# Cross-attention and a routed FFN: GpSimd's expert program unrolled to the indirect transfers alone, ScalarE addressing the bias itself

## The chip, the cores and the metric

One NeuronCore of one Trainium2 chip runs the kernel. The metric is the device time of one execution in microseconds (us). The same kernel was run three times before the change, and the median of these runs is what a changed kernel is held against.

## The reference, cut to what matters

64 sequences of 128 rows with 256 columns pass through two layers. First comes an attention whose softmax runs over the sequences, then a mixture of eight experts, of which each row (token) takes two.

```python
x = x + attention(layernorm(x), ctx_1024, ctx_1024)   # out = v @ softmax(k^T q / 16, over the batch)

# FFN: T = 8192 tokens, H = 256, F = 512, E = 8 experts, K = 2
xn = layernorm(x)
topk_logits, topk_idx = jax.lax.top_k(xn @ router_w.T, 2)
probs = jax.nn.softmax(topk_logits)
hmid = gelu(einsum('th,efh->etf', xn, w1) + b1[:, None, :])
y = einsum('etf,ehf->eth', hmid, w2) + b2[:, None, :]
out = x + einsum('eth,te->th', y, combine)            # combine holds probs at the two chosen experts
```

## The kernel before, in words

The kernel writes a separate program for each engine, and semaphores join the programs. It has three stages: the maximum and the sum of the softmax (two passes over x and ctx), the attention with the second layernorm and the choice of experts, and the experts. The change is in the third stage, and the second one only matters in that it leaves one row of 514 words per token in the DRAM table `rows_first`: the token's x (256 words), its normalized x as two f16 parts, high and low (256 words), and its two probabilities.

**Groups.** The tokens of one expert are padded to groups of 256 (`GROUP`), two tiles of 128 (`SUB`). There are 39 groups for the first choice (round 0) and 39 for the second (round 1), 78 in all (`ALL`). VectorE works out two tables in SBUF: `index`, with four columns for each group (two for the rows to read, two for the rows to write), and `owner_i`, with the expert of each group.

**Steps.** All engines walk through the same steps. In step i they work on different groups, by the lags `L_TR, L_G1, L_G2 = 2, 3, 4`:

- GpSimd (POOL in the profile) issues the two gathers of group i (L532) into one of six pairs of row buffers (`LANES`), then the two scatters of group i-4 (L540), once VectorE has raised `x_sum` for that group. Before a gather it waits until the scatter of group i-6 has landed (`x_out`), since that group had the same buffers.
- TensorE (PE) runs the 24 matmuls of the first layer of group i-3 (L680), the eight transposes of group i-2 (L691) and the 24 matmuls of the second layer of group i-4 (L703), in this order.
- ScalarE (ACT) applies Gelu to group i-3 in four calls (L1059), two after each half of the first layer (`x_hid`), then copies the transposed rows of group i-2 to SBUF as `xT` (L1067). The first layer of the next step waits for that copy.
- VectorE (DVE) splits the Gelu output into a high and a low f16 part (L952, L954), adds the output bias (L941) and adds the second layer's result to the rows (L968), which raises `x_sum`.

**What stands ahead of a gather on GpSimd.** In each step a copy takes four columns of `index` into `ring_idx` (L526), a load reads the group's expert from `owner_i` into a register (L528), and a second copy takes that expert's four bias columns out of `b1T` into `ring_b1` (L529) and raises `x_b1`. The first gather then waits for the first copy. The gathers and scatters take their indices from `ring_idx`. ScalarE waits for `x_b1` and reads its bias at a fixed place in `ring_b1`. TensorE and VectorE already load the expert from `owner_i` themselves (L673, L696, L937).

**Loops.** `expert_steps` writes 6 steps out, loops over five blocks of 6, writes some 12 steps around the middle out, loops over five more blocks and writes the rest out. Inside a loop the group number is a register, so that waits and addresses are computed.

**The middle.** Round 1 reads what round 0 wrote, in the table `rows_second`. The first four groups of round 1 (39 to 42) are gathered from `rows_first` for TensorE's sake. At step 43 GpSimd waits until all scatters of round 0 have landed, and gathers these four groups again from `rows_second` over three steps ("late" gathers, L520), for VectorE's sums.

In step 36 TensorE also runs 64 matmuls that list the tokens of round 1 (L664).

Of the kernel before, what the change touches and what calls it, by code (L numbers as in the profile page):

```python
# [27 lines left out]
I32 = mybir.dt.int32  # L28
U32 = mybir.dt.uint32
ALU = mybir.AluOpType  # L30
ACT = mybir.ActivationFunctionType
# [4 lines left out]
EXPERTS, HID = 8, 512  # L36
# [96 lines left out]
def xattn_ffn(nc, x, ctx, router_w, w1, b1, w2, b2, out):  # L133
# [7 lines left out]
    with ExitStack() as stack:  # L141
# [145 lines left out]
        def take(words, rows=P):  # L287
            taken[0] += words
            return slots[0:rows, taken[0] - words:taken[0]]
# [27 lines left out]
        past = take(ROUNDS * GROUPS * EXPERTS, 1)  # L317
        owner = take(ROUNDS * GROUPS, 1)
        owner_i = take(ROUNDS * GROUPS, 1).bitcast(I32)
        ring_idx = take(LANES * 2 * SUB).bitcast(I32)  # L320
        ring_b1 = take(LANES * FC)
        assert taken[0] <= 28 * 2 * ROW
        b2_all = take(EXPERTS * DIM)
        assert taken[0] <= 28 * 2 * ROW
# [9 lines left out]
        x_rows_in = sems("x_rows_in", LANES)  # L334
        x_late_in = sems("x_late_in", L_G2)
        x_out = sems("x_out", LANES)
        x_idx = sem("x_idx")
        x_b1 = sem("x_b1")
        x_tr = sem("x_tr")
        x_xT = sem("x_xT")  # L340
        x_hid = sem("x_hid")
# [100 lines left out]
        def _(pool):  # L442
# [58 lines left out]

            for r in range(RING):
                pool.wait_ge(a_stored[r], 16 * (PAIRS // RING))
            pool.wait_ge(r_owner, 1)
            pool.wait_ge(r_index, 1)

            def group(i, k, n, rnd):
                if is_step(i, k, GROUPS):
                    pool.wait_ge(r_index, 2)
                if is_step(i, k, GROUPS + L_G2):  # L510
                    for r in range(LANES):
                        pool.wait_ge(x_out[r], 32 * len(range(r, GROUPS, LANES)))
                if isinstance(i, int):

                    for g in late_loads(i + k):
                        r = g % LANES
                        pool.wait_ge(x_rows_in[r], 32 * len(range(r, g + 1, LANES)))
                        pool.wait_ge(x_tr, g + 1)
                        for s in range(SUB):
                            pool.indirect_dma_start(row_buf[r * SUB + s], None, table[1],  # L520
                                                    bass.IndirectOffsetOnAxis(ap=ring_idx[:, r * 4 + s:r * 4 + s + 1], axis=0)).then_inc(x_late_in[g - GROUPS], 16)
                if live(i, k, 0, ALL):
                    g, r = i + k, k % LANES
                    source = table[1] if round_of(i, k, 0, rnd) == 1 and not is_late(g) else table[0]
                    after(pool, x_out[r], n * 32 + k // LANES * 32)
                    pool.tensor_copy(ring_idx[:, r * 4:r * 4 + 4], index[:, bass.ds(g * 4, 4)]).then_inc(x_idx, 1)  # L526
                    pool.wait_ge(x_idx, 1)
                    e = pool.value_load(owner_i[0:1, bass.ds(g, 1)], min_val=0, max_val=EXPERTS - 1)  # L528
                    pool.tensor_copy(ring_b1[:, r * FC:(r + 1) * FC], b1T[:].rearrange("p e f -> p (e f)")[:, bass.ds(e * FC, FC)]).then_inc(x_b1, 1)  # L529
                    wait_apart(pool, x_idx, g + 1)  # L530
                    for s in range(SUB):
                        pool.indirect_dma_start(row_buf[r * SUB + s], None, source,  # L532
                                                bass.IndirectOffsetOnAxis(ap=ring_idx[:, r * 4 + s:r * 4 + s + 1], axis=0)).then_inc(x_rows_in[r], 16)
                if live(i, k, L_G2, ALL):
                    g, r = i + k - L_G2, (k - L_G2) % LANES
                    first = round_of(i, k, L_G2, rnd) == 0
                    wait_apart(pool, x_sum, g + 1)
                    for s in range(SUB):
                        rows = row_buf[r * SUB + s] if first else row_buf[r * SUB + s][:, X2:X2 + DIM]
                        pool.indirect_dma_start(table[1] if first else out_rows, bass.IndirectOffsetOnAxis(ap=ring_idx[:, r * 4 + 2 + s:r * 4 + 3 + s], axis=0), rows, None,  # L540
                                                bounds_check=TOKENS - 1, oob_is_err=False).then_inc(x_out[r], 16)
            expert_steps(pool, group)
            for r in range(LANES):
                pool.wait_ge(x_out[r], 32 * len(range(r, ALL, LANES)))

# [440 lines left out]
        def _(act):  # L986
# [59 lines left out]
            act.activation(b2_all, b2_all, ACT.Copy, scale=WSCALE).then_inc(r_b2s, 1)  # L1046

            act.activation(warm[:], neg_half[:, 0:1], ACT.Gelu)


            def group(i, k, n, rnd):
                if live(i, k, L_G1, ALL):
                    g, r, r2 = i + k - L_G1, (k - L_G1) % LANES, (k - L_G1) % 2
                    act.wait_ge(x_b1, g + 1)
                    after(act, x_low, g * 2 - 2)
                    for f in range(FC):
                        if f % 2 == 0:
                            act.wait_ge(x_hid, g * 2 + f // 2 + 1)
                        last = act.activation(act32[r2][:, f * GROUP:(f + 1) * GROUP], psum[:, 2 + 2 * r2 + f // 2, (f % 2) * GROUP:(f % 2 + 1) * GROUP],  # L1059
                                              ACT.Gelu, bias=ring_b1[:, r * FC + f:r * FC + f + 1], scale=1.0 / WSCALE)  # L1060
                        if f % 2:
                            last.then_inc(x_act, 1)
                if live(i, k, L_TR, ALL):
# [24 lines left out]
```

## Time and profile before

| | us |
|---|---|
| median of 3 runs | 858.28 |
| lowest and highest run | 855.77, 863.21 |
| span of the profiled execution | 909.8 |
| experts' stage in it, from the first gather to the end | 327.2 to 909.8 |

The profiled execution has no time of its own beside its span, which runs from its first to its last instruction. The span is 51.5 us above the median of the runs, so that the profile describes a slower execution than the ones that are timed. Times in the profile count from the start of the span. "Idle before" is the time an engine stood still ahead of an instruction, and the name behind the arrow is what ended it: "issue" means that nothing was waited for that the profile shows, and "remote" that the semaphore was raised later than the end of any instruction that the profile has for it.

### The profile page before, as it was taken

What the parts mean: (1) busy time and instruction counts of PE and PEld (TensorE: products, weight loads), DVE (VectorE), ACT (ScalarE), POOL (GpSimd) and SP (SyncE); (2) the same over time, 40 slices, a digit from 0 to 9 for tenths busy, and PEclk for the clock granted to TensorE, in tenths of its full rate; (3) what the DMA queues carried; (4) which work ended last, traced back from release to release, by engine and by line L of the source; (5) the groups of instructions that cost most, each with busy time, mean ns of one, the idle gap of its engine ahead of it and who ended that gap; (6) DMA issues with size and microseconds to landing.
All of it is one profiled execution on the core that took longest, in us unless ns stands there. A gap on an engine that the chain in (4) does not pass through costs nothing. (4 is left out here: it accounts for less than half of the span.)

```text
span 909.8 us, 22499 instructions
## 1 busy us (share of the span) xinstructions
PE 770.1 (85%) x5931; PEld 649.5 (71%) x5932; DVE 622.8 (68%) x1520; ACT 390.1 (43%) x715; POOL 574.0 (63%) x815
## 2 busy tenths in 40 slices
PE   6999996999996449888989887989588889879886
PEld 5678885878885338766877776978367778767775
DVE  6998999899998758655655654363465656556554
ACT  3555664576666204333333433143133333334331
POOL 5664776788884056666576566366766666665663
PEclk9999997999997559999999999799789999999998
DMA  7887773488885124444344443343533343333330
GB/s 227 251 250 240 237 228 114 137 269 266 267 275 192 53 60 134 131 147 157 118 148 156 142 133 119 112 140 76 159 106 111 106 129 108 97 115 116 96 107 2
DMA packets 82200, 137.20 MB, mean 151 GB/s; under 512 B 10075, under 2 KB 55140, under 8 KB 82032
## 3 DMA queue, kind: packets, MB, share of 16 engines
q0 software_dynamic: 23104, 68.43, 24.9%
q1 hardware_dynamic: 59056, 68.26, 23.9%
q8 instruction: 22, 0.36, 0.2%
q14 instruction: 18, 0.15, 0.1%
HBM read 94.56 MB, written 47.59 MB: 156 GB/s over the span
## 5 line engine op out<-in xcount | busy, mean ns | idle before, releaser
L680 PE MATMUL psum<-work,w1T_high 128*128 128x256 f16 x1248 | 227.4, 285 | 53.5 <-ACT work L1067 36.6
L1059 ACT ACTIVATE work<-psum,slots 128x256 f32<-128x256 f32 x312 | 130.2, 471 | 309.4 <-PE psum L680 233.0
L703 PE MATMUL psum<-w2T_high,slots 128*128 x1248 | 214.7, 277 | 6.2 <-issue 5.1
L680 PEld LDWEIGHTS psum<-work,w1T_high 128*128 x1248 | 124.0, 102 | 85.9 <-issue 67.2
L680 PE MATMUL psum<-work,w1T_low 128*128 128x256 f16 x624 | 177.6, 285 | 3.5 <-issue 3.5
L703 PE MATMUL psum<-w2T_low,slots 128*128 x624 | 172.4, 276 | 1.7 <-issue 1.7
L952 DVE CAST slots<-work 128x512 f16<-128x512 f32 x156 | 71.0, 455 | 138.4 <-ACT work L1059 114.8
L703 PEld LDWEIGHTS psum<-w2T_high,slots 128*128 128x128 f16 x1248 | 119.6, 99 | 23.2 <-issue 9.2
L561 PE MATMUL psum<-slots,work 128*128 (+1 forms) x512 | 124.0, 392 | 7.4 <-ACT slots L991 6.8
L540 POOL DMA_INDIRECT rows_second<-slots x78 | 82.3, 1055 | 66.0 <-issue 35.6
L968 DVE SCALAR_TENSOR_TENSOR slots<-psum,slots 128x256 f32<-128x256 f32 x156 | 68.2, 478 | 78.5 <-remote 63.9
L540 POOL DMA_INDIRECT out_x<-slots x78 | 83.4, 1069 | 57.9 <-issue 44.9
L532 POOL DMA_INDIRECT slots<-rows_first,slots x86 | 90.0, 1047 | 45.8 <-issue 45.6
L561 PEld LDWEIGHTS psum<-slots,work 128*128 128x128 f32 x512 | 94.4, 193 | 32.1 <-issue 15.5
L954 DVE TENSOR_TENSOR slots<-work,slots 128x512 f16<-128x512 f32 x156 | 109.5, 702 | 5.4
L1067 ACT ACTIVATE work<-psum 128x1024 f16<-128x1024 f16 x78 | 80.0, 1026 | 77.3 <-remote 42.2
L532 POOL DMA_INDIRECT slots<-rows_second,slots x70 | 71.6, 1022 | 38.4 <-issue 38.4
L941 DVE SCALAR_TENSOR_TENSOR slots<-slots 128x256 f32<-128x256 f32 x156 | 69.2, 485 | 25.9 <-issue 21.3
L680 PEld LDWEIGHTS psum<-work,w1T_low 128*128 x624 | 63.8, 102 | 15.0 <-issue 5.5
L703 PEld LDWEIGHTS psum<-w2T_low,slots 128*128 128x128 f16 x624 | 61.8, 99 | 11.8 <-issue 4.1
L633 PE MATMUL psum<-slots,work 128*128 (+1 forms) x256 | 65.5, 400 | 4.3 <-DVE slots L832 4.3
L691 PE MATMUL psum<-ident,slots 128*128 128x128 f16 x624 | 50.9, 224 | 19.8 <-DMA slots<-rows_first,slots 11.5
(126 smaller groups left out, 1125.2 us busy)
## 6 DMA issues: line engine op xcount, KB each, us to landing
work<-in_ctx SPq DMA_DIRECT2D x96, 256.0 KB, 3.5
rows_first<-slots SPq DMA_DIRECT2D x32, 514.0 KB, 3.9
slots<-in_x SPq DMA_DIRECT2D x32, 256.0 KB, 3.8
work<-in_L_ffn_w SPq DMA_DIRECT2D x32, 256.0 KB, 3.2
work<-in_x SPq DMA_DIRECT2D x32, 256.0 KB, 3.1
slots<-rows_first,slots POOLq DMA_INDIRECT x86
rows_second<-slots POOLq DMA_INDIRECT x78
slots<-rows_second,slots POOLq DMA_INDIRECT x78
```

What stands on the lines that cost most here:

```text
L532: pool.indirect_dma_start(row_buf[r * SUB + s], None, source, bass.IndirectOffsetOnAxis(ap=ring_idx[:, r * 4 + s:r * 4 + s + 1], axis=0)). ...
L540: pool.indirect_dma_start(table[1] if first else out_rows, bass.IndirectOffsetOnAxis(ap=ring_idx[:, r * 4 + 2 + s:r * 4 + 3 + s], axis=0), ...
L561: mm = pe.matmul(psum[:, r2, h * DIM:(h + 1) * DIM], ctx_ring[:, place, h * P:(h + 1) * P], slot(b, 0, DIM), start=True, stop=True)
L633: mm = pe.matmul(psum[:, 2 + r, j * DIM:(j + 1) * DIM], a_ctxT[:, 2 * r + j, h * P:(h + 1) * P], slot(m * 2 + j, h * DIM, DIM), start=(h = ...
L680: mm = pe.matmul(h, w1T[pw][:, f, c, bass.ds(e * P, P)], xT[r2][:, (px * HC + c) * GROUP:(px * HC + c + 1) * GROUP], start=(c == 0 and px ...
L703: mm = pe.matmul(y, act16[r2][pa][:, f * GROUP + s * P:f * GROUP + (s + 1) * P], w2T[pw][:, f, bass.ds(e * DIM, DIM)], start=(f == 0 and p ...
L941: last = dve.scalar_tensor_tensor(rows[:, X2:X2 + DIM], b2_all[:, bass.ds(e * DIM, DIM)], rows[:, PR + now:PR + now + 1], rows[:, X2:X2 + ...
L952: dve.tensor_copy(act16[r2][0][:, cols], act32[r2][:, cols]).then_inc(x_high, 1)
L954: dve.tensor_tensor(act16[r2][1][:, cols], act32[r2][:, cols], act16[r2][0][:, cols], ALU.subtract).then_inc(x_low, 1)
L968: last = dve.scalar_tensor_tensor(rows[:, X2:X2 + DIM], psum[:, 6 + r2, s * DIM:(s + 1) * DIM], rows[:, PR + now:PR + now + 1], rows[:, X2 ...
L1059: last = act.activation(act32[r2][:, f * GROUP:(f + 1) * GROUP], psum[:, 2 + 2 * r2 + f // 2, (f % 2) * GROUP:(f % 2 + 1) * GROUP], ACT.Ge ...
L1067: act.activation(xT[r2], psum[:, 0, :].bitcast(F16), ACT.Copy).then_inc(x_xT, 1)
```

## The change

- GpSimd's program for the experts is written out for all 82 steps, with no loop and no register. The two copies (L526, L529), the expert's load (L528) and the buffers `ring_idx` and `ring_b1` are gone. Gathers and scatters read their indices from `index` in place. The order of gathers, scatters and late gathers is the same.
- ScalarE loads the expert from `owner_i` for each group and addresses the bias in `b1T` by that register. Its wait for `x_b1` is gone. Ahead of the stage it waits once for `owner_i` and `b1T`.
- GpSimd no longer waits for `r_owner`; the semaphores `x_idx` and `x_b1` are gone.

```diff
-            def group(i, k, n, rnd):
-                if is_step(i, k, GROUPS):
+            def gather(g, s, source, landed_on):
+
+                pool.indirect_dma_start(row_buf[g % LANES * SUB + s], None, source,
+                                        bass.IndirectOffsetOnAxis(ap=index[:, g * 4 + s:g * 4 + s + 1], axis=0)).then_inc(landed_on, 16)
+
+            for step in range(ALL + L_G2):
+                if step == GROUPS:
                     pool.wait_ge(r_index, 2)
...
-                if live(i, k, 0, ALL):
-                    g, r = i + k, k % LANES
-                    source = table[1] if round_of(i, k, 0, rnd) == 1 and not is_late(g) else table[0]
-                    after(pool, x_out[r], n * 32 + k // LANES * 32)
-                    pool.tensor_copy(ring_idx[:, r * 4:r * 4 + 4], index[:, bass.ds(g * 4, 4)]).then_inc(x_idx, 1)
-                    pool.wait_ge(x_idx, 1)
-                    e = pool.value_load(owner_i[0:1, bass.ds(g, 1)], min_val=0, max_val=EXPERTS - 1)
-                    pool.tensor_copy(ring_b1[:, r * FC:(r + 1) * FC], b1T[:].rearrange("p e f -> p (e f)")[:, bass.ds(e * FC, FC)]).then_inc(x_b1, 1)
-                    wait_apart(pool, x_idx, g + 1)
+                if step < ALL:
+                    g = step
+                    after(pool, x_out[g % LANES], g // LANES * 32)
                     for s in range(SUB):
-                        pool.indirect_dma_start(row_buf[r * SUB + s], None, source,
-                                                bass.IndirectOffsetOnAxis(ap=ring_idx[:, r * 4 + s:r * 4 + s + 1], axis=0)).then_inc(x_rows_in[r], 16)
+                        gather(g, s, table[1] if g >= GROUPS + L_G2 else table[0], x_rows_in[g % LANES])
...
             def group(i, k, n, rnd):
                 if live(i, k, L_G1, ALL):
                     g, r, r2 = i + k - L_G1, (k - L_G1) % LANES, (k - L_G1) % 2
-                    act.wait_ge(x_b1, g + 1)
+                    e = act.value_load(owner_i[0:1, bass.ds(g, 1)], min_val=0, max_val=EXPERTS - 1)
                     after(act, x_low, g * 2 - 2)
...
-                                              ACT.Gelu, bias=ring_b1[:, r * FC + f:r * FC + f + 1], scale=1.0 / WSCALE)
+                                              ACT.Gelu, bias=b1T[:].rearrange("p e f -> p (e f)")[:, bass.ds(e * FC + f, 1)], scale=1.0 / WSCALE)
```

GpSimd's program in one step of the first loop, before. L526 to L529 are the copies and the expert's load ("TENSOR_LOAD slots" reads `owner_i`, which lies in the tensor `slots`), L532 the gathers, L540 the scatters.

```order
L526 COPY slots<-slots 128x4
L528 ISA
L528 TENSOR_LOAD slots
L528 ISA x2
L529 ISA
L529 COPY slots<-b1T 128x4
L118 REGISTER_ALU
L532 DMA slots<-rows_first,slots 128x514 x2
L118 REGISTER_ALU
L540 DMA rows_second<-slots 8192x514 x2
```

GpSimd's program from the start of the stage, after. L504 is the gather and L529 the scatter.

```order
L504 DMA slots<-rows_first,slots 128x514 x10
L529 DMA rows_second<-slots 8192x514 x2
L504 DMA slots<-rows_first,slots 128x514 x2
L529 DMA rows_second<-slots 8192x514 x2
L504 DMA slots<-rows_first,slots 128x514 x2
```

Nothing but the four transfers of a step is left, and the scatters of one step are followed directly by the gathers of the next.

ScalarE's program in one step of the first loop, before. L1059 is Gelu, L1067 the copy to `xT`.

```order
L1058 REGISTER_ALU
L1059 ACTIVATE work<-psum,slots 128x256 x2
L1058 REGISTER_ALU
L1059 ACTIVATE work<-psum,slots 128x256 x2
L1065 REGISTER_ALU
L111 ISA
L1067 ACTIVATE work<-psum 128x1024
```

ScalarE's program in one step of the first loop, after. L1049 is Gelu, L1057 the copy to `xT`, L1044 the expert's load.

```order
L1044 ISA
L1044 TENSOR_LOAD slots
L1044 ISA x2
L1048 REGISTER_ALU
L1049 ISA
L1049 ACTIVATE work<-psum,b1T 128x256
L1049 ISA
L1049 ACTIVATE work<-psum,b1T 128x256
L1048 REGISTER_ALU
L1049 ISA
L1049 ACTIVATE work<-psum,b1T 128x256
```

The load of the expert has moved from GpSimd to ScalarE, where it stands behind the copy to `xT` of the step before, and each Gelu has an address instruction ahead of it.

## Rows read from the trace of the kernel before

**Rows 1.** The page's first part: busy time, share of the span, instructions.
```profile
PE 770.1 (85%) x5931; PEld 649.5 (71%) x5932; DVE 622.8 (68%) x1520; ACT 390.1 (43%) x715; POOL 574.0 (63%) x815
```
**Rows 2.** Groups by line: POOL's of the experts (busy, mean ns, idle before).
```profile
L532 POOL DMA_INDIRECT slots<-rows_first,slots x86 | 90.0, 1047 | 45.8 <-issue 45.6
L532 POOL DMA_INDIRECT slots<-rows_second,slots x70 | 71.6, 1022 | 38.4 <-issue 38.4
L540 POOL DMA_INDIRECT rows_second<-slots x78 | 82.3, 1055 | 66.0 <-issue 35.6 <-DVE slots L968 30.4
L540 POOL DMA_INDIRECT out_x<-slots x78 | 83.4, 1069 | 57.9 <-issue 44.9 <-DVE slots L968 13.0
```
**Rows 3.** Timeline of POOL from 505 us: start, length, line, idle before.
```profile
505.02 1.02 POOL L540 DMA_INDIRECT rows_second<-slots  x1 [1.90 <-DVE slots L968]
506.35 1.00 POOL L540 DMA_INDIRECT rows_second<-slots  x1 [0.30 <-issue]
507.34 0.21 POOL L526 COPY slots<-slots 128x4 int32 x1
507.47 0.20 POOL L529 COPY slots<-b1T 128x4 f32 x1
508.39 1.00 POOL L532 DMA_INDIRECT slots<-rows_first,slots  x1 [0.72 <-issue]
...
513.29 0.30 POOL L526 COPY slots<-slots 128x4 int32 x1
```
**Rows 4.** Timeline of TensorE, 502 to 508 us.
```profile
502.24 0.39 PE L680 MATMUL psum<-work,w1T_high 128*128 128x256 f16 x2 [1.26 <-ACT work L1067]
...
507.93 0.27 PE L680 MATMUL psum<-work,w1T_high 128*128 128x256 f16 x1
```
**Rows 5.** Timeline of POOL: first and last of 42 scatters right behind a gather.
```profile
357.91 1.02 POOL L540 DMA_INDIRECT rows_second<-slots  x1 [0.31 <-issue]
...
875.58 1.02 POOL L540 DMA_INDIRECT out_x<-slots  x1 [0.30 <-issue]
```
**Rows 6.** Waits from 337 to 906 us: engine, line, releaser, us, times, longest.
```profile
DVE slots L968 <- remote: 63.9, 22, 6.0
ACT work L1059 <- remote: 56.3, 15, 11.5
ACT work L1067 <- remote: 42.2, 22, 3.7
PE psum L680 <- ACT work L1067: 35.4, 20, 3.3
```
**Rows 7.** The source view of L532: who waited for the gathers.
```profile
  PE psum L691: 17.0, 2
```
**Rows 8.** Timeline of POOL: the first gather, and a scatter of the last steps.
```profile
327.21 1.23 POOL L532 DMA_INDIRECT slots<-rows_first,slots  x1 [0.78 <-issue]
...
889.76 1.00 POOL L540 DMA_INDIRECT out_x<-slots  x1 [5.55 <-DVE slots L968]
```
**Rows 9.** Timeline of POOL in the middle: the first late gather, the next gathers.
```profile
631.74 0.99 POOL L520 DMA_INDIRECT slots<-rows_second,slots  x1 [2.01 <-issue]
...
655.14 0.97 POOL L532 DMA_INDIRECT slots<-rows_second,slots  x1 [0.81 <-issue]
```
**Rows 10.** The source views of L937 and L941: VectorE's load of the expert.
```profile
L937 DVEq TENSOR_LOAD <-slots x78: 300/306/590, 342.6 to 897.7; - x78
L941 DVEq FUSED_REGOPS  x78: 69/75/76, 343.5 to 898.3; - x78
```
**Rows 11.** Timeline of ScalarE, 505 to 510 us.
```profile
505.80 1.02 ACT L1067 ACTIVATE work<-psum 128x1024 f16<-128x1024 f16 x1
509.44 0.84 ACT L1059 ACTIVATE work<-psum,slots 128x256 f32<-128x256 f32 x2 [2.62 <-issue]
```
**Rows 12.** The page's third part: a queue, its packets, MB, share of 16 engines.
```profile
q8 instruction: 22, 0.36, 0.2%
```
**Rows 13.** Timeline of VectorE, 505 to 507 us.
```profile
505.94 0.43 DVE L952 CAST slots<-work 128x512 f16<-128x512 f32 x1 [0.16 <-ACT work L1059]
```

More of the change, by code:

```diff
@@ L319, in xattn_ffn @@
         owner_i = take(ROUNDS * GROUPS, 1).bitcast(I32)
-        ring_idx = take(LANES * 2 * SUB).bitcast(I32)
-        ring_b1 = take(LANES * FC)
         assert taken[0] <= 28 * 2 * ROW
@@ L336, in xattn_ffn @@
         x_out = sems("x_out", LANES)
-        x_idx = sem("x_idx")
-        x_b1 = sem("x_b1")
         x_tr = sem("x_tr")
@@ L503, in _ @@
                 pool.wait_ge(a_stored[r], 16 * (PAIRS // RING))
-            pool.wait_ge(r_owner, 1)
             pool.wait_ge(r_index, 1)
-            def group(i, k, n, rnd):
-                if is_step(i, k, GROUPS):
+            def gather(g, s, source, landed_on):
[3 more added lines that the diff above has]
+                if step == GROUPS:
@@ L509, in group @@
                     pool.wait_ge(r_index, 2)
-                if is_step(i, k, GROUPS + L_G2):
+                if step == GROUPS + L_G2:
                     for r in range(LANES):
                         pool.wait_ge(x_out[r], 32 * len(range(r, GROUPS, LANES)))
[L513 to L521, printed above, removed]
@@ L534, in group @@
[L534 to L537, printed above, removed]
+                for g in late_loads(step):
+                    pool.wait_ge(x_rows_in[g % LANES], 32 * (g // LANES + 1))
+                    pool.wait_ge(x_tr, g + 1)
+                    for s in range(SUB):
+                        gather(g, s, table[1], x_late_in[g - GROUPS])
+                if step < ALL:
+                    g = step
+                    after(pool, x_out[g % LANES], g // LANES * 32)
+                    for s in range(SUB):
+                        gather(g, s, table[1] if g >= GROUPS + L_G2 else table[0], x_rows_in[g % LANES])
@@ L538, in group @@
+                if step >= L_G2:
+                    g = step - L_G2
+                    r, first = g % LANES, g < GROUPS
+                    pool.wait_ge(x_sum, g + 1)
                     for s in range(SUB):
                         rows = row_buf[r * SUB + s] if first else row_buf[r * SUB + s][:, X2:X2 + DIM]
-                        pool.indirect_dma_start(table[1] if first else out_rows, bass.IndirectOffsetOnAxis(ap=ring_idx[:, r * 4 + 2 + s:r * 4 + 3 + s], axis=0), rows, None,
+                        pool.indirect_dma_start(table[1] if first else out_rows, bass.IndirectOffsetOnAxis(ap=index[:, g * 4 + 2 + s:g * 4 + 3 + s], axis=0), rows, None,
@@ L541, in group @@
                                                 bounds_check=TOKENS - 1, oob_is_err=False).then_inc(x_out[r], 16)
-            expert_steps(pool, group)
             for r in range(LANES):
@@ L1048, in _ @@
             act.activation(warm[:], neg_half[:, 0:1], ACT.Gelu)
+            act.wait_ge(r_owner, 1)
+            act.wait_ge(s_setc, 1)
             def group(i, k, n, rnd):
```

## The prediction, made before the changed kernel was run

> **What bounds the kernel now.** I read four views, in this order: the page's busy shares, the groups by line, the timelines of single engines in the experts' stage, and the waits of that stage.
>
> The shares name TensorE (85%) and leave GpSimd at 63% [rows 1]. That is an average over three stages and does not count issue time. The experts' stage runs from GpSimd's first gather at 327.2 us [rows 8] to the end of the span at 909.8, so it is almost two thirds of the time. In it two engines have to be held against the number of steps, 78.
>
> TensorE: where nothing holds it up, one step takes 507.93 - 502.24 = 5.69 us, from the first matmul of one first layer to that of the next [rows 4].
>
> GpSimd: the groups by line give four transfer calls a step, of (90.0 + 71.6 + 82.3 + 83.4) / 312 = 1.05 us on average [rows 2]. Between two calls without a wait lie 0.30 us [rows 3]. Between a scatter's end and the next gather lie the copies and the load: from 507.35 to 508.39, 1.04 us [rows 3]. As a mean over all steps: the idle time before gathers is 45.8 + 38.4 = 84.2 us; 78 second gathers take 0.30 each, 23.4, which leaves 60.8 / 78 = 0.78 before a first gather, and the two copies ahead of it span 0.33 (507.34 to 507.67) [rows 2, 3]. That is 1.11 us. So GpSimd's own work in a step is 4 x 1.05 + 3 x 0.30 + 1.11 = 6.21 us. The shortest step that rows show is 513.29 - 507.34 = 5.95 [rows 3]. GpSimd, with its low busy share, needs half a microsecond more for a step than TensorE.
>
> Does it set the pace? In the profiled execution only partly. 78 steps of 6.21 and eight late gathers of some 1.3 (the first one starts at 631.74) [rows 9] are 495 us, out of 582.6 from 327.2 to the end. In 42 of 78 steps the first scatter starts 0.30 us behind the gather, which means that VectorE's sum had been ready and GpSimd was the late one [rows 5]; in the others GpSimd waited, as in the 1.90 us ahead of 505.02 [rows 3]. TensorE itself waited for gathered rows only 17.0 us in two places [rows 7]. What lengthens the other steps are "remote" waits: 63.9, 56.3 and 42.2 us on VectorE and ScalarE, each for a result of TensorE [rows 6].
>
> *The Trainium skill, "Perfetto Trace Analysis", section on the TensorE instruction, says that the end of a matmul in the profile is estimated and its semaphore is raised when PSUM has acknowledged the writes. By that rule a remote wait is a real lateness of TensorE that its rows hide. The trace agrees in so far as the waiting engines do start late; whether the runs without a profiler have it, no page tells.*
>
> Here I have to choose. The runs are 51.5 us shorter than the profiled span. I take most of that to come out of the remote waits (162.4 us in sum, in parts beside each other). GpSimd's stage is 582.6 us with 495 of own work, 88 of waiting. Take 51.5 off, and 36 us of waiting are left. Some 20 of these are at the two ends and in the middle, where it must wait for others anyway (2.01 before the first late gather, 5.55 at 889.76) [rows 8, 9]. So in the timed runs GpSimd would be late in nearly every step, at 6.21 + 16 / 74 = 6.4 us a step.
>
> **The change part by part.**
>
> *Copies, load and the wait ahead of a gather go.* Of the 1.11 us between a scatter and a gather 0.30 stay. GpSimd saves 0.81 us a step, 63 us over 78, and its own step becomes 4 x 1.05 + 4 x 0.30 = 5.40 us. Nothing new is waited for: `index` is complete before the first gather. What is late next is TensorE, at 5.69. So a step in which GpSimd set the pace gains 6.21 - 5.69 = 0.52 us and not 0.81. Where GpSimd was not late, the step gains nothing. Steps that gain: at least the 42 that the trace shows, 42 x 0.52 = 22 us; at most some 72 (all but those at the ends), 37 us. I take 24, near the lower end, because 42 is what was seen and because small waits stay that two engines of nearly equal pace (5.40 and 5.69) cause each other.
>
> *The middle.* After the barrier GpSimd does six transfers a step for three steps; the gather of group 45 starts at 655.14 us, 23.4 after the first late one [rows 9]. Each of these steps is GpSimd's own and gains the whole 0.81: 2.4 us.
>
> *The first gather.* One copy pair and load ahead of the first gather go, about 1 us. I count 0 to 1 and take 0.5.
>
> *ScalarE's load of the expert.* The trace has no such load on ScalarE, but VectorE has the same one: 0.306 us, and 0.19 in the middle of its register operations, which do not occupy the engine [rows 10]. It stands behind the copy to `xT` and ahead of the next Gelu. Between the end of that copy at 506.82 and the next Gelu at 509.44 ScalarE stood still for 2.62 us [rows 11]. That gap hides it: cost 0. If the cover were gone, it would be 0.5 us in each step, 39 us. TensorE's next step waits for the copy, which is ahead of the load, so I see nothing that would take the cover away.
>
> *Four bias addresses.* An address operation takes 0.075 us on VectorE [rows 10]. It stands between the wait and the Gelu, so each half starts some 0.1 later; queued behind the second half is the copy to `xT`, and TensorE waits for that. The copy ended at 506.82 and TensorE began at 507.93 [rows 4, 11]: 1.1 us of cover in an undisturbed step. In the 20 places where TensorE did wait for the copy [rows 6] it is not covered: 20 x 0.1 = 2 us, at most 20 x 0.2 = 4. Below nothing only by the wait for `x_b1` that goes; its copy is made three steps ahead, so 0. I take 1.5, since fewer such places are left in the timed runs.
>
> *The loop on GpSimd goes.* Its program grows from blocks of 24 transfers to some 320 in a row, and has to be fetched. The instruction queue moved 22 packets in 0.2% of 16 engines' span [rows 12]: 0.002 x 909.8 x 16 / 22 = 1.3 us each, an estimate. Some 20 more, each waited for in full, would be 26 us; each beside a running call, nothing. Each call is 1 us of cover and the fetch is in sequence. I take 0 and keep 26 as the far end.
>
> *VectorE's casts beside denser calls.* A cast starts at 505.94 [rows 13], inside the scatter call that ran from 505.02 and took 1.02 us; the next call took 1.00 [rows 3]. So I add nothing.
>
> *The Trainium skill, "SBUF — State Buffer", "SBUF: two separate sides", says that GpSimd cannot write transfer descriptors while VectorE runs a copy that takes the shared port. By that rule two casts of 0.455 us a step would stretch GpSimd's step from 5.40 to 6.3 us and leave no gain. The trace speaks against it here: the call with a cast inside it and the call behind it have one length.*
>
> **The sum.** 24 + 2.4 + 0.5 - 1.5 = 25.4 us less. From the median of 858.3: **833 us**. For the profiled execution, whose span is 909.8, the same sum gives 884.
>
> **The rivals.**
>
> *The change is hidden (no change).* If the 51.5 us between profile and runs lie somewhere else, TensorE's late results set the pace in the runs too, and GpSimd only follows. For it: TensorE waited for rows just twice [rows 7], and where GpSimd waited it could be for 1.9 us, with nothing of its own late [rows 3]. Against it: a late GpSimd in 42 steps. Left would be the middle, 2.4 + 0.5 - 1.5: 857 us.
>
> *All of it falls to TensorE (a larger gain).* If the remote waits are the profiler's alone, every step comes down from 6.4 to 5.69: 0.7 x 72 = 50 us, less the small waits: 815 us. Against it: two engines 0.3 us apart do not run without waits.
>
> *The transfers get in TensorE's way (slower).* ScalarE's copy had 22 remote waits with 42.2 us, 1.9 each [rows 6]. They occur in the stage in which GpSimd issues transfers without end, and today a pause of 1.1 us parts the calls in each step; without it four and more stand together. Against it speaks only that no row ties a late result to a transfer. If the density of transfers is what makes TensorE late, and not the profiler, the 36 steps that were spared get such a wait, 36 x 1.9 = 68 us, of which the 25 of the gain and some 1.1 us of cover a step (40) are to be taken off: about 3 us; if the cover is used up already, which the profiled mean of 582.6 / 78 = 7.5 us a step suggests, it is +15 to +25. It decides from the point where a step's wait exceeds the 0.5 us of gain. Time: 875 us.
>
> **How the numbers follow.** Forecast (GpSimd's pace gives way to TensorE's, 822 to 846): 0.58. Hidden: 0.20. Larger gain: 0.10. Slower: 0.12, in which I count the fetch of instructions. About 1% is what a measurement of this kernel tells from no change. Faster by over 1% (below 849.7): 0.58 + 0.10 + a little of the hidden case, 0.70. Slower by over 1%: 0.10. Within: 0.20. The range reaches from the larger gain to the hidden case with its spread: 816 to 862; beyond it lie most of the slower case and the lowest of the larger one.
>
> **What would show it.** Right: no copies on GpSimd, 0.30 us between every scatter and the next gather, waits for VectorE ahead of most scatters, and more TensorE steps of 5.69. ScalarE's load between copy and Gelu with no later start of the copy. Wrong: gaps of GpSimd over 0.30 with "issue" that come at regular places (fetching), calls longer than 1.05 (the port), remote waits of over 162 us in sum (density), or a first layer that starts later behind ScalarE's copy.

## The result, and the profile after

| | kernel before | changed kernel |
|---|---|---|
| median, us | 857.81 (855.77 to 863.21, 4 runs) | 813.97 (811.98 to 817.22, 4 runs) |
| ratio of the times | | 0.9483, 95% interval 0.9443 to 0.9524 |
| profiled execution: time, span | no time, 909.8 | 815.25, 813.4 |

The change saves 43.8 us, about 5%. 833 us was predicted, with a range of 816 to 862: the direction was right, the size too small, and the result lies 2 us below the range.

The page of the changed kernel, its shares and its groups of GpSimd (to be held against [rows 1, 2]), and the two queues that fetch instructions (the first is that of [rows 12]):

```profile
PE 742.4 (91%) x5931; PEld 647.9 (80%) x5932; DVE 618.6 (76%) x1520; ACT 386.7 (48%) x716; POOL 538.4 (66%) x658
...
L504 POOL DMA_INDIRECT slots<-rows_first,slots x86 | 89.2, 1038 | 61.5 <-DVE slots L901 35.7
L529 POOL DMA_INDIRECT rows_second<-slots x78 | 83.3, 1068 | 56.1 <-issue 34.8
L529 POOL DMA_INDIRECT out_x<-slots x78 | 82.2, 1054 | 42.1 <-issue 32.1
L504 POOL DMA_INDIRECT slots<-rows_second,slots x78 | 77.6, 995 | 25.5 <-issue 24.2
```

```profile
q8 instruction: 22, 0.36, 0.2%
q14 instruction: 19, 0.16, 0.1%
```

The calls are as long as before (1.04 us on average, 1.05 before), and GpSimd has 157 instructions less (815 to 658). One instruction queue has 22 packets in every kernel of this study; the other has 19 here, and 18 in both traces of the kernel before. The idle time ahead of second-table gathers fell from 38.4 us for 70 calls to 25.5 for 78 (here the eight late gathers are among them). Of the 61.5 us ahead of first-table gathers, 35.7 are one wait for VectorE's tables ahead of the stage, which in the kernel before stands ahead of the first copy. The idle time ahead of scatters is now GpSimd's slack.

The timeline of the changed kernel's POOL from 499 us (as [rows 3]):

```profile
499.77 1.00 POOL L529 DMA_INDIRECT rows_second<-slots  x1 [0.30 <-issue]
501.07 0.99 POOL L504 DMA_INDIRECT slots<-rows_first,slots  x1 [0.30 <-issue]
502.37 0.98 POOL L504 DMA_INDIRECT slots<-rows_first,slots  x1 [0.30 <-issue]
503.86 1.05 POOL L529 DMA_INDIRECT rows_second<-slots  x1 [0.50 <-issue]
```

0.30 us stand between a scatter and the next gather where [rows 3] has 1.04. The idle time has moved ahead of the first scatter (0.50 here; on average, by the groups above, 56.1 + 42.1 less 78 x 0.30, over 78: 0.96 us), where GpSimd waits for `x_sum`. GpSimd now waits for the others.

TensorE's timeline shows the pace. The first rows of the first layers of two neighbouring steps, and between them the transposes that follow the first one:

```profile
501.87 0.38 PE L668 MATMUL psum<-work,w1T_high 128*128 128x256 f16 x2
...
504.49 0.61 PE L679 MATMUL psum<-ident,slots 128*128 128x128 f16 x8
...
507.56 0.38 PE L668 MATMUL psum<-work,w1T_high 128*128 128x256 f16 x2
```

507.56 - 501.87 = 5.69 us, the undisturbed step of [rows 4], and no row between them has an idle time. Taken over the whole stage (the start of each first layer less the start of the one before), only 6 of the 77 differences are over 5.75 us, and every other one is 5.69.

The waits of the changed kernel between 337 and 810 us (as [rows 6]):

```profile
ACT work L1049 <- PE psum L668: 259.9, 155, 14.8
...
POOL rows_second L529 <- issue: 34.8, 75, 1.0
...
PE psum L668 <- ACT work L1057: 1.2, 1, 1.2
```

There is no remote wait, and TensorE waits once, 1.2 us, for ScalarE's copy; it waited 20 times and 35.4 us in [rows 6]. This raised the first question, whether [rows 6] describes the runs that were timed.

### The profile page after: what moved, and what is told of

Its sections match the earlier page's. It is cut to its first block and busy times, and to the rows that moved or that the text cites. A ratio compares the mean times of both kernels' runs of the same rounds, so it can differ in the third digit from the quotient of the medians.

```text
span 813.4 us, 22177 instructions
## 1 busy us (share of the span) xinstructions
PE 742.4 (91%) x5931; PEld 647.9 (80%) x5932; DVE 618.6 (76%) x1520; ACT 386.7 (48%) x716; POOL 538.4 (66%) x658
## 5 line engine op out<-in xcount | busy, mean ns | idle before, releaser
L1049 ACT ACTIVATE work<-psum,b1T 128x256 f32<-128x256 f32 x312 | 130.7, 470 | 260.0 <-PE psum L668 259.9
L668 PE MATMUL psum<-work,w1T_high 128*128 128x256 f16 x1248 | 213.3, 276 | 2.5 <-ACT work L1057 2.5
L691 PE MATMUL psum<-w2T_high,slots 128*128 x1248 | 211.1, 275 | 0.5 <-issue 0.5
L668 PE MATMUL psum<-work,w1T_low 128*128 128x256 f16 x624 | 172.4, 276 | 0.0
L940 DVE CAST slots<-work 128x512 f16<-128x512 f32 x156 | 68.8, 441 | 118.8 <-ACT work L1049 118.7
L504 POOL DMA_INDIRECT slots<-rows_first,slots x86 | 89.2, 1038 | 61.5 <-DVE slots L901 35.7
L529 POOL DMA_INDIRECT rows_second<-slots x78 | 83.3, 1068 | 56.1 <-issue 34.8
L942 DVE TENSOR_TENSOR slots<-work,slots 128x512 f16<-128x512 f32 x156 | 108.6, 696 | 5.4
L529 POOL DMA_INDIRECT out_x<-slots x78 | 82.2, 1054 | 42.1 <-issue 32.1
L1057 ACT ACTIVATE work<-psum 128x1024 f16<-128x1024 f16 x78 | 79.8, 1023 | 32.0 <-PE psum L679 32.0
L504 POOL DMA_INDIRECT slots<-rows_second,slots x78 | 77.6, 995 | 25.5 <-issue 24.2
L929 DVE SCALAR_TENSOR_TENSOR slots<-slots 128x256 f32<-128x256 f32 x156 | 68.8, 483 | 27.7 <-DMA slots<-rows_second,slots 13.4
L668 PEld LDWEIGHTS psum<-work,w1T_low 128*128 x624 | 61.9, 99 | 7.9
L478 POOL TENSOR_TENSOR smax<-slots,smax 128x768 f32<-128x768 f32 x31 | 52.3, 1686 | 19.1 <-ACT slots L986 17.2
```

The lines of the kernel that those rows point to most:

```text
L504: pool.indirect_dma_start(row_buf[g % LANES * SUB + s], None, source, bass.IndirectOffsetOnAxis(ap=index[:, g * 4 + s:g * 4 + s + 1], axis ...
L668: mm = pe.matmul(h, w1T[pw][:, f, c, bass.ds(e * P, P)], xT[r2][:, (px * HC + c) * GROUP:(px * HC + c + 1) * GROUP], start=(c == 0 and px ...
L691: mm = pe.matmul(y, act16[r2][pa][:, f * GROUP + s * P:f * GROUP + (s + 1) * P], w2T[pw][:, f, bass.ds(e * DIM, DIM)], start=(f == 0 and p ...
L929: last = dve.scalar_tensor_tensor(rows[:, X2:X2 + DIM], b2_all[:, bass.ds(e * DIM, DIM)], rows[:, PR + now:PR + now + 1], rows[:, X2:X2 + ...
L940: dve.tensor_copy(act16[r2][0][:, cols], act32[r2][:, cols]).then_inc(x_high, 1)
L942: dve.tensor_tensor(act16[r2][1][:, cols], act32[r2][:, cols], act16[r2][0][:, cols], ALU.subtract).then_inc(x_low, 1)
```

## The experiments

The predicted mechanism was that GpSimd saves the time of its two copies and the load. The rivals that were tested behind it are that the loop with its registers costs the time, and that the wait between the copies and the gather does. The latter is what later expectations call Theory 3: GpSimd's sequencer needs some 0.8 us to prepare an indirect transfer, does so while the previous one runs, and is kept from it by a wait that stands as an instruction of its own. In the diffs `index` and `ring_idx` stand for the full index expressions.

### The kernel before, traced again

No edit.

> The kernel before, unchanged, for a second trace. Theory A (the remote waits come from the profiler, not from the kernel): the span is again near 910 us, 50 us above the timed runs, with some 160 us of remote waits. Theory B (the traced execution of before was an odd one): the span is within 1% of the timed runs, 850 to 865 us, and the remote waits are a small part of the 162 us. Under B the step that is neither held by a remote wait would take GpSimd's own 6.2 us nearly everywhere.

Measured: 860.39 us, span 858.6, beside 859.55 for the runs of before on the same chip. Its waits from 337 to 855 us:

```profile
ACT work L1059 <- PE psum L680: 290.0, 156, 15.5
...
DVE slots L968 <- PE psum L703: 42.3, 53, 2.7
```

Its POOL, 507 to 512 us:

```profile
507.15 1.01 POOL L540 DMA_INDIRECT rows_second<-slots  x1 [0.30 <-issue]
508.47 1.00 POOL L540 DMA_INDIRECT rows_second<-slots  x1 [0.30 <-issue]
509.46 0.29 POOL L526 COPY slots<-slots 128x4 int32 x1
509.71 0.18 POOL L529 COPY slots<-b1T 128x4 f32 x1
510.84 1.00 POOL L532 DMA_INDIRECT slots<-rows_first,slots  x1 [0.96 <-issue]
```

And the first rows of two of its first layers on TensorE:

```profile
500.48 0.38 PE L680 MATMUL psum<-work,w1T_high 128*128 128x256 f16 x2
...
506.80 0.38 PE L680 MATMUL psum<-work,w1T_high 128*128 128x256 f16 x2
```

What follows. The trace that the prediction was read from shows an odd execution: no remote wait appears here, and the span agrees with the timed runs. Theory B holds. Here the scatter comes 0.30 us behind the gather in 72 of the 74 steps that have both, not in 42 (the same count in the first trace): GpSimd is late nearly everywhere, and a step takes 506.80 - 500.48 = 6.32 us. Of that, 0.96 us are a gap in which GpSimd does nothing that the profile shows, behind two copies that together span 0.43; the median of this gap over the 78 steps is 0.72. Over all steps scatter end to gather is 1.21 us on average.

The sum of what TensorE's steps take over 5.69 us is 65.1 us in this trace and 23.6 in the changed kernel's, and the difference, 41.5, is nearly the whole gain. It lies in two places:

| us over 5.69 in TensorE's steps | before, traced again | changed |
|---|---|---|
| first step | 1.5 | 1.6 |
| two steps at the listing of step 36 | 13.7 | 13.2 |
| three steps of the middle | 15.2 | 8.7 |
| all other 71 steps | 34.6 (48 of them over 5.75) | 0 |

The 48 steps lose 0.72 us each. They are fewer than the 72 in which GpSimd is late: TensorE runs eight steps of 5.69 us behind the first one and seven behind the listing, until GpSimd's lead is used up.

### The copies kept, the program written out

The changed kernel with both copies, the load and ScalarE's bias as before. The wait carries a constant.

```diff
+                    pool.tensor_copy(ring_idx, index).then_inc(x_idx, 1)
+                    e = pool.value_load(owner_i[0:1, bass.ds(g, 1)], min_val=0, max_val=EXPERTS - 1)
+                    pool.tensor_copy(ring_b1, b1T of expert e).then_inc(x_b1, 1)
+                    pool.wait_ge(x_idx, g + 1)
```

> GpSimd's program is written out for all steps, but keeps both copies and the expert's load; ScalarE as before. Theory 1 (what counts is GpSimd's own work in a step, 6.2 us against TensorE's 5.69): no gain, 850 to 860 us. Theory 2 (the loop with its registers and branches is what costs): most of the gain is there, under 835 us.

Measured: 818.73 us, ratio 0.9534 (0.9499 to 0.957). Its POOL from 511 us:

```profile
511.86 0.27 POOL L527 COPY slots<-slots 128x4 int32<-128x4 int32 x1
512.08 0.18 POOL L529 COPY slots<-b1T 128x4 f32 x1
512.41 1.01 POOL L509 DMA_INDIRECT slots<-rows_first,slots  x1 [0.15 <-issue]
```

What follows. By the recorded alternatives this is Theory 2, the loop; the runs below show that it is not the loop. It falsifies the prediction's reading of the gap. All that GpSimd was to be relieved of is still there, and so is most of the gain: 859.55 - 818.73 = 40.8 us of 43.8. The copies still span 0.40 us, but the gather comes 0.15 behind them instead of 0.96 (0.72 in [rows 3]; the medians over 78 steps are 0.16 and 0.72); the mean from scatter to gather is 0.64. GpSimd's own step is then 4 x 1.05 + 3 x 0.30 + 0.64 = 5.74 us, as good as TensorE's 5.69.

### The loop kept, one copy and the load off GpSimd

The kernel before with the bias on ScalarE as in the changed kernel.

```diff
-                    e = pool.value_load(owner_i[0:1, bass.ds(g, 1)], min_val=0, max_val=EXPERTS - 1)
-                    pool.tensor_copy(ring_b1, b1T of expert e).then_inc(x_b1, 1)
...
-                    act.wait_ge(x_b1, g + 1)
+                    e = act.value_load(owner_i[0:1, bass.ds(g, 1)], min_val=0, max_val=EXPERTS - 1)
```

> GpSimd keeps its loop and the copy of the indices with its wait; the bias copy and the load go and ScalarE addresses the bias itself, as in the changed kernel. Theory 1: GpSimd saves the 0.13 to 0.2 us that the second copy adds behind the first, 10 to 15 us over 78 steps: 842 to 850 us. Theory 2 (the load in front of the gather is the costly part): GpSimd's gap from scatter to gather falls below 0.7 us and the time below 830 us. A theory in which ScalarE's part costs: slower than the kernel with everything on GpSimd, over 858 us.

Measured: 854.46 us, ratio 0.9936 (0.9903 to 0.9969). Its POOL, 510 to 513 us:

```profile
510.97 0.29 POOL L526 COPY slots<-slots 128x4 int32 x1
512.11 1.15 POOL L530 DMA_INDIRECT slots<-rows_first,slots  x1 [0.84 <-POOL slots L526]
```

What follows. None of the three recorded alternatives came (842 to 850, under 830, over 858 us). One of the two copies and the load went, and the gap stayed: 0.84 us behind the one copy that is left, and 1.20 from scatter to gather on average against 1.21. The gain is 0.6%, less than the forecast held to be told from no change, though the interval leaves 1 out.

### The program written out, with the index copy alone

The changed kernel with the first copy and its wait put back; ScalarE as in the changed kernel.

```diff
+                    pool.tensor_copy(ring_idx, index).then_inc(x_idx, 1)
+                    pool.wait_ge(x_idx, g + 1)
```

> The changed kernel with the copy of the indices and its wait put back, so that GpSimd's program is unrolled and each first gather waits for one small copy. Theory 1: the gap from scatter to gather is again about 0.9 us, GpSimd's step 6.0, and the time 840 to 850 us. Theory 2 (loop or load are what costs): within 5 us of 814.

Measured: 817.48 us, ratio 0.9517 (0.9486 to 0.9548). Its POOL from 510 us:

```profile
510.67 0.49 POOL L527 COPY slots<-slots 128x4 int32<-128x4 int32 x1
511.43 1.00 POOL L509 DMA_INDIRECT slots<-rows_first,slots  x1 [0.27 <-POOL slots L527]
```

What follows. Against the run before it the work is the same (index copy, wait, gather), only the loop is missing, and 0.27 us stand where 0.84 stood. So it is the loop, or something that comes with it. In the loop a wait against a register is made of two lines, `eng.wait_ge(sem, 1)` and `eng.wait_ge(sem, count)` in `wait_apart` (L118 to L121), and one of the two stands in the program as an instruction of its own, while the gather carries the other. In the trace of the kernel of 854.46 us the own instruction starts 33 to 35 ns behind the end of the index copy in all 78 steps, so it is the one that the copy holds up. From the end of the copy to the gather it is never under 0.82 us there (median 0.84); in this kernel, where the gather carries the only wait, the median is 0.28. The before kernel has it in its written-out steps too, and the gap with it ([rows 9]: 0.81 at 655.14).

### The same with one more wait line, still no loop

The first kernel with the copies kept (818.73 us), with one line added. It changes nothing that is computed or waited for, since the second line asks for at least as much.

```diff
                     pool.tensor_copy(ring_b1, b1T of expert e).then_inc(x_b1, 1)
+                    pool.wait_ge(x_idx, 1)
                     pool.wait_ge(x_idx, g + 1)
```

> The unrolled program with both copies (e1), but ahead of the gather the wait for the index copy stands twice, so that one of the two is a sequencer instruction of its own, as in the kernel before. Theory 3 (the kernel before lost its time to that wait of its own: GpSimd's sequencer prepares a transfer for some 0.8 us, and behind a wait of its own it can begin only when the copy is done): the gap from scatter to gather goes from 0.64 back to 1.2 us, GpSimd's step to 6.2 to 6.4, and the time to 845 to 862 us, although nothing is looped. Theory 2 (loop, registers and branches): 815 to 822 us, as e1.

Measured: 858.18 us, ratio 0.9972 (0.995 to 0.9994), against 0.9534 without the line. Its POOL from 511 us:

```profile
512.22 0.30 POOL L527 COPY slots<-slots 128x4 int32<-128x4 int32 x1
512.47 0.18 POOL L529 COPY slots<-b1T 128x4 f32 x1
513.37 1.10 POOL L509 DMA_INDIRECT slots<-rows_first,slots  x1 [0.72 <-issue]
```

The source view of the wait's line in this kernel (median ns, first and last start), an instruction of GpSimd's sequencer that the kernel without the extra line has nowhere:

```profile
L531 POOLq EVENT_SEMAPHORE  x78: 17/17/17, 326.7 to 831.0; - x78
```

What follows. One wait line 78 times brings the whole cost back: 0.9972 - 0.9534 = 0.0438 of 859 us, 38 us, or half a microsecond a step. The instruction takes 17 ns by the profile; the price is in the gap behind it, 0.72 us where 0.15 stood (1.23 on average from scatter to gather, 0.64 without the line). This program has no loop and no branch, and its group numbers are constants, so none of these costs anything that the runs can tell.

### The wait moved ahead of the bias copy

The kernel before; the wait for the index copy stands between the two copies, so that the bias copy stands behind it and can run beside the preparation.

```diff
-                    pool.tensor_copy(ring_b1, b1T of expert e).then_inc(x_b1, 1)
                     wait_apart(pool, x_idx, g + 1)
+                    pool.tensor_copy(ring_b1, b1T of expert e).then_inc(x_b1, 1)
```

> The kernel before with its loop; the wait for the index copy is moved from the gather to the bias copy that stands ahead of it, so that the gather carries no wait. Theory 3: the wait is still a sequencer instruction of its own ahead of the gather, so the 0.8 us of preparation still follow it: gap 1.1 to 1.3 us, 850 to 862 us. A theory in which only a wait that the gather itself carries costs: gap near 0.6, under 830 us.

Measured: 866.3 us, ratio 1.0085 (1.0056 to 1.0113). Its POOL from 510 us:

```profile
510.47 0.29 POOL L526 COPY slots<-slots 128x4 int32 x1
510.99 0.51 POOL L530 COPY slots<-b1T 128x4 f32 x1 [0.23 <-POOL slots L526]
511.99 1.50 POOL L532 DMA_INDIRECT slots<-rows_first,slots  x1 [0.49 <-issue]
```

What follows. Behind the wait everything starts over: 0.23 us until the bias copy starts, which is now longer, and 0.49 more to the gather. From the end of the index copy, where the wait is met, to the gather it is 511.99 - 510.76 = 1.23 us, more than the 1.09 (509.75 to 510.84) of the kernel before. Part of the preparation hides under the copy (0.49 against 0.96), but the chain is longer. On average scatter end to gather is 1.36 us against 1.21. So a wait that the gather doesn't carry costs as well when another instruction stands between; the recorded range (850 to 862 us, a gap of 1.1 to 1.3) was missed by 4 us: it did not count that the bias copy would wait and take longer.

### ScalarE's load twice

The changed kernel with the expert's load written twice on ScalarE.

```diff
                     e = act.value_load(owner_i[0:1, bass.ds(g, 1)], min_val=0, max_val=EXPERTS - 1)
+                    e = act.value_load(owner_i[0:1, bass.ds(g, 1)], min_val=0, max_val=EXPERTS - 1)
```

> The changed kernel with ScalarE's load of the expert made twice in each step. If the load is hidden behind the wait for TensorE, as the prediction put it: 812 to 817 us, no change. If ScalarE's added instructions are on the path: 0.5 us in each of 78 steps, 850 us.

Measured: 815.92 us, ratio 0.9485 (0.9442 to 0.9528); the changed kernel has 0.9483. The source view of the load in the changed kernel, and of the bias addresses:

```profile
L1044 ACTq TENSOR_LOAD <-slots x78: 273/286/594, 334.2 to 794.4; - x78
```

```profile
L1049 ACTq FUSED_REGOPS  x312: 46/46/52, 338.1 to 799.7; - x156
```

And the idle time ahead of Gelu, first in the changed kernel, then with two loads:

```profile
503.48 0.84 ACT L1049 ACTIVATE work<-psum,b1T 128x256 f32<-128x256 f32 x2 [2.62 <-PE psum L668]
```

```profile
504.85 0.84 ACT L1050 ACTIVATE work<-psum,b1T 128x256 f32<-128x256 f32 x2 [2.63 <-PE psum L668]
```

What follows. The load is hidden in ScalarE's wait for TensorE, even a second time: 2.62 and 2.63 us, as in [rows 11]. This half of the change costs nothing.

### Waits that are always met

The changed kernel, with two waits ahead of each gather for semaphores that were raised long before.

```diff
                     g = step
                     after(pool, x_out[g % LANES], g // LANES * 32)
+                    pool.wait_ge(r_index, 1)
+                    pool.wait_ge(r_owner, 1)
```

> The changed kernel with two more waits ahead of each gather, on semaphores that were raised long before the stage, so that waits of their own stand ahead of the gather but are met at once. Theory 3 (a wait of its own costs only by what the sequencer can't prepare while it stands at it): no gap over 0.30 us is added, 812 to 818 us. A theory in which a wait instruction ahead of a transfer costs by itself: GpSimd's gap grows by some 0.8 us, 845 us or more.

Measured: 815.15 us, ratio 0.9479 (0.9425 to 0.9533). Its POOL from 504 us:

```profile
504.69 1.17 POOL L531 DMA_INDIRECT rows_second<-slots  x1 [0.30 <-issue]
506.17 1.00 POOL L504 DMA_INDIRECT slots<-rows_first,slots  x1 [0.30 <-issue]
```

What follows. The trace has one wait instruction a step here (78), so a wait of its own is there; it is already met and passes while a scatter runs. It costs nothing, and the gather comes 0.30 us behind the scatter. The cost needs both: the wait as an instruction of its own ahead of the transfer, and a semaphore that is raised only by the work just issued.

### Can the rest be had? The late gathers, one group a step

What the changed kernel's TensorE still loses is in the middle and at the listing (below). In the middle GpSimd does six transfers a step for three steps. The changed kernel was given one late group in each of four steps instead.

```diff
-            first = step - L_G2 + (step > GROUPS + L_G2)
-            return [g for g in range(first, step - L_G2 + 2) if is_late(g) and step >= GROUPS + L_G2]
+            return [g for g in (step - L_G2,) if is_late(g)]
```

> The changed kernel with the four late gathers one per step (steps 43 to 46) instead of two in step 43 and one each in 44 and 45; an attempt at a faster middle. If the 9 us that the middle costs over TensorE's own steps come from the gather of group 43 standing behind four late transfers: 2 to 4 us less, 810 to 812. If they come from GpSimd's six transfers a step as such: no change, 812 to 817. If group 40's late rows are what TensorE waits for: 2 to 4 us more.

Measured: 828.82 us, ratio 0.965 (0.9619 to 0.9681), 14.9 us slower than the changed kernel. Its POOL in the middle:

```profile
590.51 1.22 POOL L528 DMA_INDIRECT out_x<-slots  x1 [3.74 <-issue]
...
613.29 1.27 POOL L528 DMA_INDIRECT out_x<-slots  x1 [3.79 <-issue]
```

The same stretch in the changed kernel:

```profile
592.80 1.28 POOL L529 DMA_INDIRECT out_x<-slots  x1 [1.11 <-issue]
...
600.87 1.02 POOL L529 DMA_INDIRECT out_x<-slots  x1 [0.30 <-issue]
```

What follows. None of the recorded sizes came (2 to 4 us either way, or no change). GpSimd stands 3.7 to 4.1 us before the scatters of four steps: with one late group a step, its rows are fetched in the very step that needs them. The rows of the scatter say only "issue"; who waits for the late rows is VectorE, three times with up to 7.7 us, as the waits of this kernel from 580 to 620 us have it (13.4 us in the same window of the changed kernel), and the scatters wait for VectorE's sums:

```profile
DVE slots L928 <- DMA slots<-rows_second,slots: 22.7, 3, 7.7
```

Six transfers in a row, all 0.30 us apart, are the better order. No version here beats the changed kernel.

## Why the prediction was wrong in size and right in direction

**The term that was mis-sized** is the first one of the sum: "at least the 42 that the trace shows, 42 x 0.52 = 22 us; at most some 72, 37 us. I take 24". The table of the second trace gives 34.6 us for it: 48 of TensorE's steps were held up, by 0.72 us each. Both factors were low. The gap between scatter and gather was 1.21 us on average and not 1.11, which makes GpSimd's own step 4.2 + 0.9 + 1.21 = 6.31 us, and the 24 steps from 391.4 to 544.8 us take 6.39 on average. The second term was low too: the middle was put at 2.4 us and gave TensorE 15.2 - 8.7 = 6.5. The forecast counted its steps in a trace that it had already called slower than the timed runs.

The prediction had worked out 6.4 us for a timed step and 0.7 x 72 = 50 for it, but only inside a rival with 0.10. That rival, "all of it falls to TensorE", gave 815 us. Its pace was right; that its total came so near is partly luck, since 48 steps gained and not 72, the middle gave more than it had, and its condition fails: the remote waits aren't the profiler's, as the second trace has the profiler and none of them.

**The reading of [rows 6]** was wrong. 162.4 us of remote waits, and the many steps in which GpSimd was not late, belong to one execution. They are in no other trace of this study, neither of this kernel nor of a changed one (no remote wait in the ten others). The reason to stay at 24, that "small waits stay", does not hold either: 4 x 1.04 + 4 x 0.30 = 5.36 us of GpSimd beside 5.69 of TensorE run without a wait on TensorE. What made that execution late stays open.

**The cause of the gap** was wrong, though its size was nearly right. The idle time between scatter and gather was priced as the copies and the load; the wait was named beside them and had no price of its own. With all of them in place and the wait carried by the gather 41 of the 44 us are gained (818.73 us), and with one wait of its own added nearly nothing is (858.18, ratio 0.9972). The copies and the load themselves are worth some 0.9534 - 0.9483, 4.4 us, and those two intervals overlap. By the forecast's reasoning a part of the change that takes the copies away and keeps the wait would have gained; the run with one copy and the load taken away gained 5 us (3 to 8 by its interval).

**Right, by its steps.** TensorE's step of 5.69 us is now the bound, as the prediction said. ScalarE's load is hidden, and its addresses take 46 ns each: 1.5 us were taken for them, and the ordinary steps of 5.69 us show none. The written-out program costs no fetch that the time shows: 858.18 with it against 859.24 with the loop. The prediction looked for some 20 more packets in the queue of [rows 12], which has 22 in every kernel; the other instruction queue has 19 in the changed kernel and 23 in the one of 858.18 us, against 18.

VectorE's work beside denser calls does not lengthen the mean call (1.04 us, 1.05 before), as forecast. That it is free is not shown, though: in the changed kernel the calls that overlap one of VectorE's subtractions of the low part (L942) by over 0.15 us take 1.07 us on average and the ones that overlap none 1.00, leaving out two calls of over 1.5; in the second trace of before it is 1.10 and 1.02. Whether VectorE is the cause was not tested.

By GpSimd's clock the middle gained less than forecast: group 45 is gathered 606.10 - 584.21 = 21.9 us after the first late gather, against 23.4 in [rows 9], 1.5 where 2.4 were taken. The half microsecond forecast for the first gather can't be told: it starts at 327.64 us here and at 329.60 in the second trace of before, but at 325.20 and 329.57 in the kernels of 828.82 and 815.92 us, whose programs ahead of that gather are those of the changed one. The slower rival (dense transfers make TensorE late) fell with the remote waits, and the hidden one with the 72 steps.

Two rows of the changed kernel, of its POOL in the middle, are the source of the 21.9:

```profile
584.21 0.99 POOL L504 DMA_INDIRECT slots<-rows_second,slots  x1 [2.00 <-issue]
...
606.10 1.16 POOL L504 DMA_INDIRECT slots<-rows_second,slots  x1 [0.30 <-issue]
```

**What is left.** Of the 23.6 us that six steps take over 5.69, 13.2 lie at the listing of step 36 and 8.7 in the middle. TensorE's timeline in the changed kernel:

```profile
530.30 11.02 PE L652 MATMUL psum<-slots 128*128 128x78 f16 x64
541.14 0.61 PE L668 MATMUL psum<-work,w1T_high 128*128 128x256 f16 x2
...
546.16 0.61 PE L679 MATMUL psum<-ident,slots 128*128 128x128 f16 x8
...
549.23 0.38 PE L668 MATMUL psum<-work,w1T_high 128*128 128x256 f16 x2
```

And its windows there (length, busy time of PE, PEld, DVE, ACT, POOL with instructions, granted clock, DMA share, GB/s):

```profile
535.00:541.00 6.00, 6.00 (x37) 6.00 (x36) 0.00 (x0) 0.00 (x0) 2.06 (x3) 0.57 0.46 139
541.00:545.00 4.00, 4.00 (x22) 2.87 (x21) 0.00 (x0) 0.84 (x2) 0.00 (x0) 0.50 0.00 0
```

64 matmuls of 78 columns take 541.14 - 530.30 = 10.8 us. TensorE has been busy without a pause ahead of that (22.0 of 22.0 us from 513 to 535, at a granted clock of 1.00). While they run, the granted clock falls to a mean of 0.57 in the stretch from 535, and from 541 to 545 it is 0.50, the level of 1.2 GHz. The first layer that follows takes 546.16 - 541.14 = 5.02 us instead of 504.49 - 501.87 = 2.62, which costs 2.4. Both are in the kernel before as well (13.7 us over 5.69 in its second trace), and the change does not touch them.

## What to carry to other kernels

Ahead of an indirect transfer on GpSimd put no separate wait instruction that only the instruction just issued will meet; let the transfer carry it, or better, take away what it waits for. Read a gap marked "issue" as a question, not as the time of the instructions named beside it, and test it by adding one such instruction rather than by taking the work away. Where a profiled span and the timed runs disagree by 6%, take the steps and their count from a second trace before multiplying with them.

## What the runs showed of the hardware

- From the end of the index copy to the indirect call it takes at least 0.80 us where a wait instruction of its own stands between (medians 0.85, 0.84 and 0.84 in the second trace of before and the kernels of 854.46 and 858.18 us). Where the call itself carries the wait the medians are 0.29 and 0.28 (818.73 and 817.48 us), with some calls later. A wait instruction of 17 ns costs half a microsecond a step in this way, 38 us over 78.
- Where the condition is met long before, the wait instruction costs nothing (815.15 us): the call starts 0.30 us behind the 1.0 us of the call before.
- That GpSimd's sequencer prepares a call in that time, and does so beside the running call unless a wait stops it, is the reading that fits all these runs. What the sequencer does in it, the profile doesn't show.
- The same delay appears where a register instruction carries the wait. In the changed kernel the wait for `x_sum` is carried by a register move of the scatter, and where that scatter is late it starts a median of 0.82 us behind the move (0.78 to 1.07, 65 times). There it costs nothing, as GpSimd has time to spare.
- What a loop costs by itself is bounded from one side only: 858.18 written out against 859.24 in a loop, both with the wait. No run has the loop and a gather that carries its only wait.
- One execution in a trace can be quite unlike the timed ones: 909.8 us against 858.6 in a second trace of the same kernel, with TensorE's semaphores late by up to 11.5 us at places that the second one does not show. Its cause is open.
